# Softmax attention in a two-layer tower: maxima products over 64 rows, even and odd heads side by side

## The reference, cut to what matters

```python
xh = x.reshape(b, n, h, hd)                       # 4, 1024, 12, 16
qkv = jnp.einsum('bnhd,hde->bnhe', xh, W_qkv) + b_qkv
q, k, v = jnp.split(qkv, 3, axis=-1)
scores = jnp.einsum('bihd,bjhd->bhij', q, k) / jnp.asarray(f, x.dtype) ** 0.5
p = jax.nn.softmax(scores, axis=-1)
attn = jnp.einsum('bhij,bjhd->bihd', p, v)
out = attn.reshape(b, n, f) @ W_out + b_out
```

## Time and profile before

| | |
|---|---|
| device time, median of 3 runs | 1805.18 us (1803.73 to 1810.18) |
| device time of the profiled execution | 1795.51 us |
| its span, first to last instruction | 1793.9 us |
| mean granted TensorE clock | 0.923 of 2.4 GHz |
| busy over the span: TensorE / VectorE / ScalarE / GpSimd | 89% / 61% / 35% / 24% |
| embedding and projection | about 0 to 109 us |
| first maxima, without steps | 109.5 to 160.7 us |
| the 192 steps | 160.7 to about 729 us |
| experts, relu attention, experts | the rest |

### The profile page before, as it was taken

One profiled execution on the slowest core, in us unless ns is written; L12 is line 12 of the kernel. 1 busy time (PEld: TensorE's weight loads), 2 busy tenths in 40 slices (PEclk: granted clock), 3 DMA queues, 4 the chain that ended last, 5 costly groups with the idle time before them and its releaser, 6 DMA issues. The chain is left out here.

```text
span 1793.9 us, 28354 instructions
## 1 busy us (share of the span) xinstructions
PE 1596.3 (89%) x8964; PEld 865.2 (48%) x8965; DVE 1090.1 (61%) x2478; ACT 627.6 (35%) x849; POOL 423.1 (24%) x518
## 2 busy tenths in 40 slices
PE   4779999999899999875999947899988989999997
PEld 2422332233233332574566634567775656666664
DVE  5978997899799893356233335565544943333336
ACT  3412666576566668410211102222123112212111
POOL 6650000000000000100455525000000226666650
PEclk9866999999999999885899977999899889999999
DMA  2470222022222200630211112000001401111116
GB/s 78 151 169 1 37 37 36 1 35 35 36 35 36 36 1 1 154 119 16 60 42 39 39 46 64 1 10 19 10 18 51 126 18 51 53 50 53 46 42 216
DMA packets 64847, 92.82 MB, mean 52 GB/s; under 512 B 9905, under 2 KB 50036, under 8 KB 63732
## 3 DMA queue, kind: packets, MB, share of 16 engines
q1 hardware_dynamic: 51520, 65.08, 15.3%
q0 software_dynamic: 12288, 25.18, 4.9%
q10 hardware_dynamic: 960, 1.57, 0.4%
HBM read 61.82 MB, written 29.98 MB: 51 GB/s over the span
## 5 line engine op out<-in xcount | busy, mean ns | idle before, releaser
L553 DVE TENSOR_REDUCE sa_half_max<-psum 128x1 f32<-128x512 f32 x768 | 494.5, 687 | 68.8 <-PE psum L656 50.0
L610 ACT ACTIVATE sa_probs<-psum 128x1024 f32<-128x1024 f32 x384 | 372.3, 1022 | 167.2 <-PE psum L647 165.7
L656 PE MATMUL psum<-k_stack,q_stack 96*128 96x512 bf16 x768 | 285.5, 410 | 19.7 <-DVE sa_half_max L553 9.6
L647 PE MATMUL psum<-q_stack,k_stack 97*128 97x512 bf16 x768 | 231.1, 385 | 6.3 <-ACT sa_probs L610 5.4
L656 PEld LDWEIGHTS psum<-k_stack,q_stack 96*128 96x128 bf16 x768 | 75.0, 98 | 274.7 <-issue 133.2
L679 PE MATMUL psum<-sa_probs,sa_v_ext 128*32 128x512 f32 x1536 | 206.6, 610 | 0.6 <-ACT sa_probs L610 0.6
L1580 PE MATMUL psum<-w_e_up_a,ex_xt 128*128 x448 | 172.5, 528 | 0.0
L1430 ACT ACTIVATE ex_silu<-psum 128x384 f32<-128x384 f32 (+1 forms) x112 | 59.3, 529 | 290.8 <-PE psum L1580 288.3
L1470 DVE COPY ex_to_rows<-slot_rows 128x2 uint32 (+1 forms) x56 | 12.8, 229 | 211.5 <-DMA y_rows<-ex_y,ex_to_rows 117.4
L1596 PE MATMUL psum<-w_e_down,ex_g_t 128*128 x752 | 137.2, 334 | 0.5 <-DVE ex_g_t L1462 0.5
L1596 PEld LDWEIGHTS psum<-w_e_down,ex_g_t 128*128 128x128 f32 x752 | 120.7, 190 | 34.5 <-issue 34.5
(11 more groups left out here) (286 smaller groups left out, 2183.1 us busy)
## 6 DMA issues: line engine op xcount, KB each, us to landing
attn<-y_rows SPq DMA_DIRECT2D x24, 384.0 KB, 4.6
q_stack<-qk_parts SPq DMA_DIRECT2D x66, 128.0 KB, 4.3
k_stack<-qk_parts SPq DMA_DIRECT2D x66, 128.0 KB, 6.6
qk_parts<-qk_split SPq DMA_DIRECT2D x16, 384.0 KB, 3.5
x_tokens<-x SPq DMA_DIRECT2D x16, 384.0 KB, 2.6
qk_parts<-qk_split SPq DMA_DIRECT2D x16, 192.0 KB, 4.4
w_e_down<-e_down SPq DMA_DIRECT2D x1, 3072.0 KB, 32.6
out<-h SPq DMA_DIRECT2D x8, 384.0 KB, 4.0
```

What stands on the lines that cost most here:

```text
L553: nc.vector.tensor_reduce(half_max[:, g, hd, qt, half:half + 1], slot, AX.X, ALU.max).then_inc(ring_free[r], 1)
L610: nc.scalar.activation(probs[:, st % 2, 2 * pair:2 * pair + 2, :], ps[:, 2 * pair:2 * pair + 2, :], ACT.Exp, scale=SCALE0).then_inc(exp_do ...
L647: last = nc.tensor.matmul(ps[:, hd, :], kst[:, g, hd, kt * P:(kt + 1) * P], qst[:, g, hd, half * HALF:(half + 1) * HALF], start=True, stop ...
L656: last = nc.tensor.matmul(ps[:, 4 + r, :], qst[0:SK, g, hd, qt * P:(qt + 1) * P], kst[0:SK, g, hd, half * 512:(half + 1) * 512], start=Tru ...
```

## The change

1. Maxima products read 64 of the 96 stacked rows: parts 0 and 1 of q with parts 0 and 1 of k. For even heads these are rows 0 to 63.
2. The stacks of odd heads are turned: part k goes to row (64 + 16 k) mod 128, so that their first four parts lie in rows 64 to 127 and the last two in rows 0 to 31; the row of the maxima is row 32 (`MAX_ODD`), rows 33 to 63 are zero. The stacks grow to 128 partitions. Scores of odd heads run over 128 rows.
3. `max_units` hands out an even and an odd head in turn, and in `ORDER` the maxima come in pairs of one even and one odd head.
4. Each stack load is split into one for the even and one for the odd heads: 24 per group, half the size each. The row of maxima is loaded in two transfers. GpSimd fills the zero rows and two rows of ones.
5. The loads of the very first group move from ScalarE's queue at the end of the embedding into SP's loop over the chunks, which is written out.

```diff
+MAX_ODD = SK - DB
+def max_rows_of(odd):
+    return slice(DB, P) if odd else slice(0, DB)
+def score_rows_of(odd):
+    return slice(0, P) if odd else slice(0, SK + 1)
+def load_stack(eng, s, b, g, which, odd):
+    stack, order = ((s.q_stack, Q_STACK), (s.k_stack, K_STACK))[which]
+    for k, part in enumerate(order):
+        row = (DB + k * HD) % P if odd else k * HD
+        src = s.qk_parts[which, part, bass.ds(b * D + g * GD, GD), :].rearrange("(s u r) t -> u r s t", u=2, r=HD)
+        eng.dma_start(stack[row:row + HD, g, odd::2, :], src[odd]).then_inc(s.loaded[g], 16)
+STACK_LOADS = 4 * len(Q_STACK)
 def load_stacks(eng, s, b, g):
-    for which, (stack, order) in enumerate(((s.q_stack, Q_STACK), (s.k_stack, K_STACK))):
-        for k, part in enumerate(order):
-            src = s.qk_parts[which, part, bass.ds(b * D + g * GD, GD), :]
-            eng.dma_start(stack[k * HD:(k + 1) * HD, g, :, :],
-                          src.rearrange("(s r) t -> r s t", r=HD)).then_inc(s.loaded[g], 16)
+    for which in range(2):
+        for odd in range(2):
+            load_stack(eng, s, b, g, which, odd)
...
-            with sp.Fori(0, B) as b:
+            for b in range(B):
...
+                    early = 2 * b + u - 3
+                    if early == 0:
+                        for w in range(2):
+                            sp.wait_ge(two["sent"][w], START + 64)
+                    if 0 <= early < 4:
+                        load_stack(sp, s, 0, 0, early // 2, early % 2)
...
-            def finish():
-                for u in range(2):
-                    act.wait_ge(two["sent"][u], START + 64)
-                load_stacks(act, s, 0, 0)
-            pipeline(act, B, start, step, finish)
+            pipeline(act, B, start, step, lambda: None)
...
-            return [("max", g, k // (2 * TB), k // 2 % TB, k % 2) for k in range(first, last)]
+            return [("max", g, k // (4 * TB) * 2 + k % 2, k // 4 % TB, k // 2 % 2) for k in range(first, last)]
...
-            sp.dma_start(qst[SK:SK + 1, g, :, :].rearrange("o s t -> o (s t)"),
-                         max_dram[g].rearrange("(o k) t -> o (k t)", o=1)).then_inc(max_loaded[g], 16)
+            rows = max_dram[g].rearrange("(o s u k) t -> u o s (k t)", o=1, u=2, k=TB)
+            for odd, row in enumerate((SK, MAX_ODD)):
+                sp.dma_start(qst[row:row + 1, g, odd::2, :], rows[odd]).then_inc(max_loaded[g], 16)
...
+            sp.wait_ge(v_init, START + 4)
             load_max(sp, 0, 0)
...
-            nc.gpsimd.memset(kst[SK:SK + 1, :, :, :], 1.0).then_inc(ones_row, 1)
-            pool.wait_ge(ones_row, START + 1)
+            nc.gpsimd.memset(qst[MAX_ODD:DB, :, 1::2, :], 0.0).then_inc(v_init, 1)
+            nc.gpsimd.memset(kst[MAX_ODD:DB, :, 1::2, :], 0.0).then_inc(v_init, 1)
+            pool.wait_ge(v_init, START + 4)
+            for odd, row in enumerate((SK, MAX_ODD)):
+                nc.gpsimd.memset(kst[row:row + 1, :, odd::2, :], 1.0).then_inc(ones_row, 1)
+            pool.wait_ge(ones_row, START + 2)
...
                 for hd in (2 * pair, 2 * pair + 1):
-                    last = nc.tensor.matmul(ps[:, hd, :], kst[:, g, hd, kt * P:(kt + 1) * P],
-                                            qst[:, g, hd, half * HALF:(half + 1) * HALF], start=True, stop=True)
+                    rows = score_rows_of(hd % 2)
+                    last = nc.tensor.matmul(ps[:, hd, :], kst[rows, g, hd, kt * P:(kt + 1) * P],
+                                            qst[rows, g, hd, half * HALF:(half + 1) * HALF], start=True, stop=True)
...
-                    last = nc.tensor.matmul(ps[:, 4 + r, :], qst[0:SK, g, hd, qt * P:(qt + 1) * P],
-                                            kst[0:SK, g, hd, half * 512:(half + 1) * 512], start=True, stop=True)
+                    rows = max_rows_of(hd % 2)
+                    last = nc.tensor.matmul(ps[:, 4 + r, :], qst[rows, g, hd, qt * P:(qt + 1) * P],
+                                            kst[rows, g, hd, half * 512:(half + 1) * 512], start=True, stop=True)
...
-            ORDER = ("scores", "maxima", "scores", "maxima", "maxima", "outputs", "maxima")
+            ORDER = ("scores", "scores", "maxima", "outputs", "maxima")
...
-                            elif left:
-                                unit = left.pop(0)
-                                ug = unit[1]
-                                if unit[2:] == (0, 0, 0):
-                                    pe.wait_ge(loaded[ug], START + 16 * LOADS * ((b if ug > g else b + 1) + 1))
-                                produce(b, unit, *uses(b, n))
-                                n += 1
+                            else:
+                                for unit in left[:2]:
+                                    ug = unit[1]
+                                    if unit[2:] == (0, 0, 0):
+                                        pe.wait_ge(loaded[ug], START + 16 * LOADS * ((b if ug > g else b + 1) + 1))
+                                    produce(b, unit, *uses(b, n))
+                                    n += 1
+                                left = left[2:]
...
-              nc.sbuf_tensor("q_stack", [SK + 1, NG, GH, S], BF16) as s.q_stack,
-              nc.sbuf_tensor("k_stack", [SK + 1, NG, GH, S], BF16) as s.k_stack,
+              nc.sbuf_tensor("q_stack", [P, NG, GH, S], BF16) as s.q_stack,
+              nc.sbuf_tensor("k_stack", [P, NG, GH, S], BF16) as s.k_stack,
```

More of the change, by code:

```diff
@@ L420, in softmax_attention @@
                                                  for n in ("inv_done", "v_init", "ones_row", "constants"))
-        LOADS = 2 * len(Q_STACK)
+        LOADS = STACK_LOADS
         block = ctx.enter_context(nc.Block())
         def max_units(g, first, last):
-            return [("max", g, k // (2 * TB), k // 2 % TB, k % 2) for k in range(first, last)]
+            return [("max", g, k // (4 * TB) * 2 + k % 2, k // 4 % TB, k // 2 % 2) for k in range(first, last)]
         UNITS = GH * TB * 2
@@ L641, in scores @@
                     pe.wait_ge(loaded[g], START + 16 * LOADS * (b + 1))
-                    pe.wait_ge(max_loaded[g], START + 16 * (b + 1))
+                    pe.wait_ge(max_loaded[g], START + 2 * 16 * (b + 1))
                 if follows is not None:
@@ L688, in _ @@
                 produce(0, unit, n % SLOTS, n // SLOTS)
-            pe.wait_ge(ones_row, START + 1)
+            pe.wait_ge(ones_row, START + 2)
             for pair in range(2):
                 scores(0, 0, 0, pair, None)
-            ORDER = ("scores", "maxima", "scores", "maxima", "maxima", "outputs", "maxima")
+            ORDER = ("scores", "scores", "maxima", "outputs", "maxima")
             def sequence(b, last):
```

## The result

| | before | after |
|---|---|---|
| device time, median | 1806.28 us (4 runs, 1803.73 to 1810.18) | 1758.74 us (4 runs, 1757.09 to 1764.99) |
| profiled execution | 1795.5 us, span 1793.9 | 1765.0 us, span 1763.3 |
| mean granted TensorE clock | 0.923 | 0.914 |

The ratio is 0.9741, with a 95% interval of 0.971 to 0.9772: 47.5 us off, where 31.2 were forecast. The forecast's sign and its main mechanism held; its size did not: 1758.74 lies outside the forecast's own range of 1762 to 1790 and 0.7 us inside the wide one (1758 to 1801).

The account below looks back on a forecast made before the run. TensorE was taken to bound the attention step, with VectorE 0.4 us behind. 37.6 - 4.7 - 2.2 + 0.5 = 31.2 us off the 1805.2 median gave 1774 us; own range 1762 to 1790, eight-in-ten range 1758 to 1801.

Parts of the forecast that it names:

- The step: Attention step on TensorE with maxima in side-by-side pairs: 2.62 us, 0.22 less than 2.84; 37.6 us over 171 steps.
- the three turns: TensorE's switches in a step between 64-row pairs and the scores or the outputs' 32-column products: 0.09 us each.
- The rivals at the step: Attention step: pairs not side by side (1842, chance 0.09); dearer turns (1800, 0.11); VectorE bound sooner (1747, 0.06).
- the first rival: A pair's products on TensorE don't run side by side, the second 0.22 behind: step 3.04, total 1842 us; chance 0.09.
- Tails: Transposes ending some attention steps: a loss of 4.7 us over 11 maxima groups and 2.2 us over 22 output cases.
- The row of maxima: Its load in two transfers of 0.24 us each in place of one: costs nothing, with 1.2 us to spare.
- SP's and GpSimd's extra work: Early attention: SP's 48 loads take 22.6 us, GpSimd's four fills some 20.7 us; all hidden.
- The moved loads: First group's stack loads moved from ScalarE's queue into SP's embedding loop: at most 0.5 us won at the first maximum.

## Why the prediction was right or wrong

- **The step: right.** 2.84 to 2.62 us, by the prices read ahead: two products side by side, 0.09 for each of the three turns, 0.215 from one bf16 product to the next, 128 rows at the price of 97. 0.22 x 171 = 37.6 us stand. (In the range, a turn dearer by 0.04 was put at 12 us; two such turns a step make 0.04 x 2 x 171 = 13.7. Nothing rests on it.)
- **The rivals at the step: none happened.** The products of a pair start 0.003 us apart in all 342 pairs of the steps, although each waits for its own slot, where the first rival would have needed 0.09; with both in one half its mechanism comes, at 0.20 a step over before as it was priced. The turns between the pair and the outputs, which no row of before showed, cost 0.09 like the others (0.32 us from pair to outputs, 0.235 of it the pair's own): the rows of the other turns were the right ones to go by. The Trainium skill (TensorEngine Tiling (Array Packing), Key Properties) says that a change of the tiling mode drains TensorE. Here that does not mean a wait until the last product is out, which would have made a turn 0.165: the outputs start 0.32 us behind the pair, whose row lasts 0.39.
- **Tails: somewhat too cheap.** With transposed maxima a step takes 3.65 us, 1.03 over 2.62, where 0.94 were reckoned; with transposed outputs 3.23, 0.61 over it for the 0.53 of the forecast. Against before that is 0.52 x 11 + 0.18 x 22 = 9.7 us for 6.9. The reason for the loss was right: the wait for the slot is in the row. The second transpose starts 205.65 - 204.39 = 1.26 us behind the pair, for the 1.15 at which its slot was put free.
- **The row of maxima: wrong, and small.** "Nothing, with 1.2 us to spare" fails in two groups, by 0.61 and 0.75 us (by 0.9 to 1.2 in the other two profiles). The forecast had two sends of 0.24 each; together they take 1.15 us, the second starting 0.61 after the first. The store's way, 209.17 - 206.57 = 2.6 us in that group, was taken from the quicker one of the earlier trace rows.
- **SP's and GpSimd's extra work: right.** 112.05 to 134.5 and 20.9 us, hidden as said.
- **The moved loads: wrong.** "At most 0.5 us to win" was read from one execution, in which ScalarE's loads landed right at the barrier. The move done alone gives 8.6 us (4.3 to 12.5), undone 7 to 12; the run of the loads alone leaves 8 at the most for it. The step that failed is to take a bound from a single start time as if it held in all executions. With whole loads only 0.3 to 2.5 us of the gain are seen between SP's last send and the first maximum, so its cause is open for the larger part, and the written-out loop of SP is not excluded.
- **The returns of the loop: not in the forecast at all.** It costed the split loads by SP's sends, "half as large", and never by what shares the DMA queues with them. Two returns, each some 6 us shorter beside its neighbours (15 steps around a return take 54.05 us before for 43.95 elsewhere, 45.64 for 41.51 after), are 11.9 us. That the split of the loads causes it is shown by the run of the loads alone, where 15 steps around a return take 47.1 and 47.0 us; whether by their size or by their slower pace is not. That it is VectorE's program waiting behind the loads' packets rests on the packets' times, which fit to 0.01 us at all eight returns with whole-size loads, and on the written-out loop, where no such packet comes and only 1.25 us of idle time are left; no run moved those packets by themselves.

So the sum by what was measured: 37.6 - 9.7 - 1.4 + 11.9 = 38.4 us in the steps (37.9 between the same two profiles, 39.4 in the mean of all five), and 8.6 for the first group's loads: 47 of the 47.5. The last term is the one whose size is not settled. The forecast's 31.2 are these without the returns, with 0.5 for the first group's loads, nothing for the row of maxima and tails a little too cheap. That the time still falls into the wide range is luck: both large terms that the forecast lacked pull the same way, and its lower end was drawn down to 1758 without a cause being named. The time at half clock (1.2 GHz) in the steps goes from 15 to 25 us in profiles with whole loads to 4 to 12 us in those of the changed kernel; it follows the returns, where TensorE stands idle, and is part of the 54.05.

## What to carry to other kernels

Price a moved or resized transfer not only by the sends that its queue makes but by all that travels at the same time, an engine's own program among it: look at each loop's return for a restart marked "issue" and for transfers that fill the queues there. Prices of turns and of products side by side may be taken from another part of the same profile, as here from fp32 products of a shared expert for bf16 ones. A start time that decides a term should be read from more than one execution.

## What the runs showed of the hardware

- The same bytes in loads of 64 KB over 16 rows and two heads, instead of 128 KB over 16 rows and four, land in 2.1 us for 4.3 to 6.6. At the returns their median packet of 2 KB takes 84 to 88 ns for 216 to 252, and while the loads run the DMA engines are busy 42 to 48% for 92 to 97%, at 118 to 132 GB/s for 129 to 155. The smaller loads are also sent at half the pace (24 in 12 us, 12 in 5.7), and no run tells the size from the pace.
- At a loop's return VectorE stands idle 7.0 to 8.9 us beside the large loads, 2.8 to 3.4 beside the small ones, and 1.25 us where the loop is written out.
- Two bf16 products of 64 rows and 512 columns start 0.003 us apart in the two halves of the rows, each behind a wait of its own, and 0.226 apart in the same half. A turn between such pairs and products of full height or of 32 output columns costs 0.09 us.
- GpSimd fills 32 rows of 6144 elements in 5.21 us, and one row of 6144 in the same (10.48 for two).
- Executions of one kernel differ by some 10 us, and a good part goes with the granted clock: the part behind the steps, the same code in all, takes 1060 to 1071 us and holds 181 to 214 us at half clock (1.2 GHz).
